# Another order of PSUM banks for two turned outputs, a gate product and two value products, and other steps for ACT's casts and the context's upper half

## What is computed

```python
xn  = rmsnorm(layernorm(x), norm_w)
q, k, v = xn @ wq.T, ctx @ wk.T, ctx @ wv.T           # 16 heads of 32
p   = softmax(where(mask, q k^T / sqrt(32), -inf))     # mask: True on the invalid tail of the context
x   = x + tanh(g_xattn) * sigmoid(xn @ wg.T) * ((p v) @ wo.T)
h   = silu(m @ w_gate) * (m @ w_up)                    # m = layernorm(x), weights unpacked from FP4
x   = x + tanh(g_ffn) * rmsnorm(h @ w_down)
```

## Time and profile before

| | us |
|---|---|
| median of 3 runs | 585.15 |
| lowest and highest of the runs | 583.78 and 585.34 |
| the profiled execution | 583.25 |
| its span in the profile | 581.4 |
| PE busy in the span | 534.2 (92%) |
| DVE, ACT, POOL busy in the span | 431.1, 347.9, 295.7 |
| chain of work that ended last | PE 64%, DVE 15%, issue 8%, ACT 8% |

### The profile page before, as it was taken

How to read it: one execution, slowest core, us unless ns; L and a number is a source line. 1 busy time by engine, 2 the same in 40 slices (tenths; PEclk the granted TensorE clock), 3 DMA queues, 4 the chain that set the end, 5 groups by cost and what they waited for, 6 DMA issues and landing times.

```text
span 581.4 us, 12493 instructions
## 1 busy us (share of the span) xinstructions
PE 534.2 (92%) x3962; PEld 468.0 (80%) x3962; DVE 431.1 (74%) x994; ACT 347.9 (60%) x948; POOL 295.7 (51%) x320
## 2 busy tenths in 40 slices
PE   2787988999899998999997898999999999999996
PEld 2687878988789887988886676888998988899983
DVE  6666868767688686896647987988897898867721
ACT  4677558645676446765467644676666667665610
POOL 6913373402735026441104854887776677866720
PEclk9998999999999999999999999999999999999998
DMA  6930146331464322432672027502110211011111
GB/s 223 340 118 0 56 130 184 135 135 49 147 168 159 117 65 93 147 132 92 220 277 76 2 61 238 195 0 83 38 36 2 83 37 37 2 37 37 37 64 32
DMA packets 27899, 59.37 MB, mean 102 GB/s; under 512 B 3656, under 2 KB 5832, under 8 KB 27848
## 3 DMA queue, kind: packets, MB, share of 16 engines
q1 hardware_dynamic: 27848, 58.76, 30.6%
HBM read 39.62 MB, written 19.14 MB: 101 GB/s over the span
## 4 chain that ended last, share of the span: by engine, by line
PE 64%; DVE 15%; issue 8%; ACT 8%; POOL 1%; DMA 1%; DVEq 0%; ACTq 0%; SPq 0%; POOLq 0%
PE bank L1771 18%; PE bank L1784 15%; PE bank L323 12%; PE bank L1620 5%; PE bank L1624 3%; PE bank L332 2%; ACT probs L928 2%; PE bank L1648 2%; DVE nmax L1206 2%; DVE vb_both L1174 2%; PE bank L1673 1%; PE bank L1659 1%; DVE part_gate L1395 1%; ACT vb_both L908 1%; DVE words L1317 1%
## 5 line engine op out<-in xcount | busy, mean ns | idle before, releaser
L1771 PE MATMUL bank<-mT_hi,wgu 128*128 128x320 f32 x440 | 138.3, 325 | 9.9 <-ACT part_up L1037 3.4
L1771 PE MATMUL bank<-mT_lo,wgu 128*128 128x320 f32 x440 | 131.2, 309 | 0.0
L733 POOL TENSOR_TENSOR o<-pv_sum,rinv 100x128 f32<-100x128 f32 x64 | 42.6, 666 | 147.4 <-DVE pv_sum L1223 147.2
L928 ACT ACTIVATE probs<-bank,nmax 100x96 f32<-100x96 f32 x256 | 66.6, 348 | 61.6 <-DVE nmax L1206 61.6
L1771 PEld LDWEIGHTS bank<-mT_hi,wgu 128*128 128x128 f32 x440 | 82.5, 188 | 23.5 <-ACT part_up L1037 5.2
L1771 PEld LDWEIGHTS bank<-mT_lo,wgu 128*128 128x128 f32 x440 | 82.7, 188 | 3.5
L805 POOL TENSOR_TENSOR part_gate<-part_gate 128x320 f32<-128x320 f32 x55 | 57.0, 1037 | 54.8 <-DVE part_gate L1395 54.8
L1037 ACT ACTIVATE part_up<-bank,scale 128x320 f32<-128x320 f32 x110 | 57.3, 522 | 39.9 <-PE bank L1771 39.6
L1395 DVE SCALAR_TENSOR_TENSOR part_up<-bank,scale,part_up 128x320 f32<-128x320 f32 x110 | 58.9, 546 | 20.0 <-ACT part_up L1037 18.5
L1037 ACT ACTIVATE part_gate<-bank,scale 128x320 f32<-128x320 f32 x110 | 52.1, 529 | 28.0 <-PE bank L1771 27.6
L1395 DVE SCALAR_TENSOR_TENSOR part_gate<-bank,scale,part_gate 128x320 f32<-128x320 f32 x110 | 55.4, 544 | 13.5 <-ACT part_gate L1037 11.8
(11 more groups left out here) (145 smaller groups left out, 1400.1 us busy)
## 6 DMA issues: line engine op xcount, KB each, us to landing
gate_up_scratch<-left SPq DMA_DIRECT2D x12, 512.0 KB, 3.7
down_scratch<-left SPq DMA_DIRECT2D x12, 512.0 KB, 2.8
wgu<-gate_up_scratch SPq DMA_DIRECT2D x11, 512.0 KB, 6.3
words<-in_packed SPq DMA_DIRECT2D x18, 256.0 KB
xn<-in_x SPq DMA_DIRECT2D x16, 200.0 KB
xa<-in_x SPq DMA_DIRECT2D x16, 200.0 KB
x_scratch<-gate SPq DMA_DIRECT2D x16, 200.0 KB
ctx_raw<-in_ctx_tail SPq DMA_DIRECT2D x4, 768.0 KB, 8.2
```

The source lines that it names most:

```text
L733: nc.gpsimd.tensor_tensor(o[hg % 2][:, :, HD * h:HD * h + HD], total[:, :, 0:HD], rinv[:, i % 4, :].unsqueeze(2).broadcast_to([L, NB, HD]) ...
L928: last = nc.scalar.activation(probs[i % 2][:, cols], SC[i % HPG][0:L, cols], ACT.Exp, bias=nmax[:, i % 4, b:b + 1])
L1771: last = nc.tensor.matmul(product_bank(j, t, i, k)[:, 0:TG], wgu[t][:, k, 128 * i:128 * i + 128], mT[j % 2][half][:, k, :], start=half == ...
```

## The change

The bank of T1 and T2 is 1 instead of 0, that of G2 is 2 instead of 1, that of A0 is 0 instead of 1 and that of A1 is 1 instead of 0 (in all three cycles of the loop; the first group's own A jobs and the last group's own T and G jobs have tables of their own that say what they said). The context's upper and lower halves are made in steps 8 (one tile), 9 (two) and 10 (one) instead of two in step 9 and two in step 10. ACT's casts of codes that fall on a step with scores (2, 6, 10 or 14) are done one step later: those of 14 and 2, in 15 and 3. POOL's products stay where they are.

```diff
-        CTX_AT = {9: (0, 1), 10: (2, 3)}
+        CTX_AT = {8: (0,), 9: (1, 2), 10: (3,)}
...
+        LEFT_AT = {at: [unit for unit in units if unit[1] > 2] for (at, _), units in DECODE_AT.items()}
+        for at in (SCORES_AT + HPG * n for n in range(HG)):
+            casts = [unit for unit in LEFT_AT.get(at, ()) if KINDS[unit[0]] == "u"]
+            LEFT_AT[at + 1] = casts + LEFT_AT.get(at + 1, [])
+            LEFT_AT[at] = [unit for unit in LEFT_AT.get(at, ()) if unit not in casts]
...
-        BANK_OF = dict(G0=0, Q3=2, G1=1, K3=0, X0=3, T1=0, G2=1, X1=0, G3=1, X2=0, X3=2, K0=1, Q0=0, T2=0, A0=1, A1=0, A2=2,
+        BANK_OF = dict(G0=0, Q3=2, G1=1, K3=0, X0=3, T1=1, G2=2, X1=0, G3=1, X2=0, X3=2, K0=1, Q0=0, T2=1, A0=0, A1=1, A2=2,
                        Q1=1, B0=3, K1=2, T3=0, B1=1, O0=1, O1=0, B2=2, Q2=1, O2=0, O3=1, K2=0, T0=1)
...
-                    for q, stage in DECODE_AT.get((i, 1), ()):
-                        if stage > 2 and KINDS[q] == "d":
+                    for q, stage in LEFT_AT.get(i, ()):
+                        if KINDS[q] == "d":
                             piece_left(cycle, q, stage - 3)
...
-                    for q, stage in DECODE_AT.get((i, 1), ()):
-                        if stage > 2 and KINDS[q] == "u":
+                    for q, stage in LEFT_AT.get(i, ()):
+                        if KINDS[q] == "u":
                             piece_left(cycle, q, stage - 3)
```

## The result

| | before | changed |
|---|---|---|
| median of 5 runs, us | 585.15 | 579.77 |
| lowest and highest | 583.78 and 586.58 | 578.01 and 580.79 |
| ratio of the runs, 95% interval | | 0.9903 [0.9881, 0.9925] |
| span of the profiled execution, us | 581.4 | 578.0 |
| one cycle of the loop, us | 74.21 | 72.72 |

The change is 5.4 us faster by the medians, 4.4 to 7.0 by the interval; 581.2 us had been forecast, with 578.8 to 584.6 as the range. The lines of the changed kernel are six higher than those of before from the diff on.

A forecast was written before the change was run, and what follows sets the result against it. PE was taken to bound the loop's cycles, busy 70.54 of 74.21 us; the walk gave 1.3 us a cycle, times three, 3.9 us, so 581.2 us on the median's scale, range 578.8 to 584.6.

The forecast's parts named there:

- T1: Step 9 on PE: T1 on bank 1 starts 0.16 us earlier, not 0.87, because POOL's o of head 7 comes next.
- X1: PE, behind T1: X1 follows G2 at once, no longer waiting for T1's lower half, and starts 0.98 us earlier in all.
- S3 behind G2's tanh: Added wait on PE from G2's bank 2: the tanh on ACT ends 0.37 us before S3 asks, so it costs nothing.
- K0: PE, behind X3: with one context tile fewer in step 10, K0 starts 1.41 us earlier in all.
- Q0's upper half: On ACT: moves earlier by between 1.19 us and PE's own 1.41; 1.3 was taken.
- Steps 11 to 0: ACT and DVE pass work to and fro, so T2's removed wait adds nothing and PE's 1.06 us at step 0 grows.
- The walk: The prediction's method: follow each removed wait through the engines' queues, valuing it only by what the next event leaves; 1.3 us a cycle.
- The casts: ACT's casts of steps 14 and 2, one step later: PE's step 0 wait shrinks 0.15 us, which S1 gives back.
- The residual: Load for O2 behind the moved store: lands near 201.3 at the latest, where DVE takes it at 201.21; costs nothing.
- residual late: Rival, chance 0.09: the load behind the moved store lands at 205.7, PE loses 1.1 us a cycle net, 588.5 us.
- The sum: All terms over the loop: 1.3 us a cycle, times three cycles, 3.9 us.
- The forecast's own bounds: Range of the forecast by itself: 579.5 to 583.6 us, 2.4 to 4.8 off, with the 0.8 by which runs scatter.

The follow-up runs named there:

- late tanh: Changed kernel with ACT's tanh of G2 put behind X1's upper half in step 9; 581.73 us in one run, cycles of 73.32 and 73.35 us.
- decoding in step 7: Changed kernel with DVE's four decoding operations of step 8 moved to the end of step 7; 580.98 us, ratio 0.9944.
- banks alone: Kernel before with only the new banks of T1, G2, T2, A0 and A1; 581.55 us, ratio 0.9927.
- casts alone: Kernel before with only ACT's casts of steps 14 and 2 moved one step later; 585.24 us, ratio 0.9992.
- maximum second: Changed kernel with DVE's row maximum of step 15 put behind the lower half of head 15; 581.11 us, ratio 0.9933.

## Why the prediction came out right, step by step

- **T1** was forecast 0.16 earlier, with POOL as the next releaser, and came 0.12 earlier with o of head 7 as releaser. The way from POOL to PE, guessed at 0.1, was 147.01 - 146.86 = 0.15. The prediction took POOL's 1.78 as given; the experiment shows that 1.4 of it is DVE's doing.
- **X1**: forecast 0.98, measured 0.96.
- **S3 behind G2's tanh**: forecast room 0.37, measured 0.35. The late tanh and the decoding in step 7 show the wait that appears when it is used up.
- **K0**: forecast 1.41, measured 1.43. Of this 0.43 was put down to the context; alone it gives 0.30, since the subtraction makes T1's lower half late while X1 still waits for it. With the new banks X1 doesn't wait for that, so the parts do better together: 1.39 for the two.
- **Q0's upper half** is where the forecast was low: I took 1.3 between 1.19 and PE's own 1.41, and it came 1.43. ACT waits 0.38 for PE there, so all of PE's gain arrives. The lower bound took DVE's run from X2's lower half on to be as long as before. It became 0.5 shorter, because a decoding instruction in it had stood beside POOL's subtraction of two tiles (158.64 to 160.62), of which one is left in step 10 (157.44 to 158.45; DVE's rows are below). The context's move does that: with the banks alone the instruction still takes 1.16.
- **Steps 11 to 0**: T2's removed wait adds nothing, as forecast, but not in the way forecast. PE was to wait longer at step 0, 1.2 to 1.4, and waits 1.02. The walk had A0 behind Q0's lower half, but not A2, whose bank the change leaves alone: A2 starts at 169.91, 0.06 behind the end of the exponentials of head 0 (168.82 + 1.03), and there PE has lost what it gained at T2. From A2 on PE and the two others have gained the same.
- **The casts**: forecast 0.15, which S1 gives back. They bring 0.10, and S1 does not give it back. It hangs on the shift of words, and that on POOL's second product, which now starts at 179.45 (last of POOL's rows above), 42.22 into the cycle instead of 43.72: 1.50 earlier. S1 is 1.49 earlier, as step 0 is, and waits 0.24 as before.
- **The residual** was to land in time (201.3 against 201.21 needed). DVE waits 1.61 for it, 1.4 more than the 0.23 that it waits at that place otherwise: the load is issued at 195.96 and used at 200.66 (SP's rows below). From the store's issue at 194.93 that is 5.7, where 3.7 for three transfers at 250 GB/s and a lead of 0.8 made 4.5. Idle on DVE at that place had been named as a sign of being wrong. It costs at most 0.04 a cycle, since DVE is idle 0.95 soon after the earlier trace rows and S2 has some 0.4 of room: the rival "residual late" had the right mechanism, but it decides from 2.1 late on (203.3 against 201.21), and this is 1.4.

DVE's decoding instruction behind X2's lower half, in the kernel before, the changed one, and the banks alone:

```profile
159.98 0.92 DVE L1326 TENSOR_SCALAR fp<-words 128x512 int32<-128x512 int32 x1
```

```profile
158.33 0.41 DVE L1332 TENSOR_SCALAR fp<-words 128x512 int32<-128x512 int32 x1
```

```profile
160.29 1.16 DVE L1332 TENSOR_SCALAR fp<-words 128x512 int32<-128x512 int32 x1
```

SP of the changed kernel, second cycle, with the store of left ahead of the finished sequence and the residual:

```profile
194.93 0.35 SPq L551 DMA_DIRECT2D gate_up_scratch<-left  x1
195.47 0.31 SPq L528 DMA_DIRECT2D x_scratch<-gate  x1
195.96 0.64 SPq L508 DMA_DIRECT2D xa<-in_x  x1
```

The sum was thus low by 0.19 a cycle: 0.13 at Q0's upper half and 0.06 net at the casts. With 1.49 instead of 1.3 it gives 3 x 1.49 = 4.5 and 580.7. The forecast's own bounds, 2.4 to 4.8 off, do not follow from its walk: 3 x 1.41 is 4.2, and nothing in the working gives 4.8. The cycle of 72.72 lies just under the 72.8 to 73.0 that had been named.

## What to carry to other kernels

Read what stands right behind each wait before giving the wait a price: here gaps of 0.87, 0.47 and 1.06 were worth 0.12, 0 and about 0.1, while the gaps of 0.65 and 0.43 were worth about their size or more (X1 gains 0.84 over T1, K0 0.42 over S3). What stands behind a wait can be a bank that the change does not name, as A2's. A chain between two other engines (step 0, S1) shows itself when the wait moves to the next place instead of going. And a step that is moved into an engine's idle time can still cost, and can give where it leaves: look at what the neighbour engine does at both times.

## What the runs showed of the hardware

**DVE and POOL hold each other up, in whole instructions.** POOL's o of head 7 takes 1.78 beside DVE's decoding and 0.40 without it; its end in the changed kernel, 146.86, lies 0.25 behind that of DVE's last decoding instruction, 146.61. Its recorded start, 145.09, lies ahead of three of the four decoding instructions (145.25, 145.59 and 145.93), so it did not get in between them. DVE's norm (0.54 for one instruction) takes 1.19 when it starts 0.11 behind POOL's subtraction of 1.02 (decoding in step 7), and 0.64 when it starts 0.65 behind one of 1.00 (the changed kernel). These are the two kernels' views of the tile xn, steps 7 and 8 (ns shortest, median, longest):

```profile
L1208 DVE TENSOR_SCALAR xn<-xn,mv,rstd x4: 535/538/1193, 140.6 to 147.3; 100x512 f32<-100x512 f32 x4
```

```profile
L1207 DVE TENSOR_SCALAR xn<-xn,mv,rstd x4: 534/542/640, 141.8 to 148.0; 100x512 f32<-100x512 f32 x4
```

If DVE goes on 0.25 before POOL's recorded end, both come out: 1.02 - 0.11 - 0.25 = 0.66 of waiting in the first case and 1.00 - 0.65 - 0.25 = 0.10 in the second. The Trainium skill (SBUF — State Buffer, "Who interferes with whom") has an exclusive lock that is held for the whole instruction, and the loser waits. These rows agree, in both directions; the prediction had taken 0.4 from it for the norm, and the row of the changed kernel has 0.10. The overlap was nearly as forecast, 1.00 - 0.65 = 0.35; the difference is mostly the 0.25 by which DVE goes on ahead of POOL's recorded end.

**A cycle can be 1.6 us longer with no edit in it.** In the third cycle of the casts alone, behind X1 (columns as in the windows above):

```profile
228.00:229.00 1.00, 1.00 (x37) 0.92 (x33) 0.59 (x3) 0.55 (x3) 1.00 (x2) 0.93 0.63 256
229.00:230.00 1.00, 1.00 (x4) 0.59 (x3) 1.00 (x3) 0.34 (x2) 1.00 (x2) 0.50 0.81 322
...
232.00:233.00 1.00, 1.00 (x5) 0.69 (x4) 0.00 (x0) 0.00 (x0) 0.36 (x1) 0.87 0.00 0
```

The granted clock is 0.50 there, 1.2 GHz instead of 2.4, for some 3.4 us, after PE had been idle for 0.88 at T1 and 0.65 at X1; the cycles before it, with nearly the same idle times (0.87 and 0.68, 0.88 and 0.69), have none of it. The same is seen in one cycle each of the maximum second (granted 0.66 from 111 to 116) and of the decoding in step 7. What sets it off in one cycle and not in the next was not tried. It is as large as the whole gain of the change in a cycle, which is why single spans are not to be compared here without the windows beside them.
